# Delta rule: the gate's statistics of three of its four sources made beside the recurrence

## The reference, cut to what matters

```python
def _per_head_stats(x):
    mean = jnp.mean(x, -1, keepdims=True)
    var = jnp.var(x, -1, keepdims=True)
    am = jnp.mean(jnp.abs(x), -1, keepdims=True)
    l2 = jnp.sqrt(jnp.sum(x * x, -1, keepdims=True))
    return jnp.concatenate([mean, var, am, l2], -1)
...
delta_out, _S = _delta_rule_chunkwise(q, k, v_direct, beta)
local_short = _fir_conv(v_direct, fir_short_w)
local_long = _fir_conv(v_direct, fir_long_w)
stats = jnp.concatenate([_per_head_stats(local_short), _per_head_stats(local_long),
                         _per_head_stats(delta_out), _per_head_stats(v_direct)], -1)
gate_in = jnp.concatenate([hs_exp, stats], -1)
h1 = jax.nn.gelu(gate_in @ mlp1_w.T + mlp1_b)
logits = h1 @ mlp2_w.T + mlp2_b
```

## Time and profile before

| | us |
|---|---|
| median of three launches | 3241.55 |
| lowest and highest of them | 3233.91 and 3244.31 |
| the profiled launch | 3234.41 |
| its span, first to last instruction | 3233.1 |
| TensorE busy in it | 2661.0 (82%) |
| VectorE busy in it | 2186.1 (68%) |
| ScalarE busy in it | 1378.1 (43%) |
| GpSimd busy in it | 572.6 (18%) |

### The profile page before, as it was taken

One profiled execution on the slowest core, in us unless ns is written; L12 is line 12 of the kernel. 1 busy time (PEld: TensorE's weight loads), 2 busy tenths in 40 slices (PEclk: granted clock), 3 DMA queues, 4 the chain that ended last, 5 costly groups with the idle time before them and its releaser, 6 DMA issues.

```text
span 3233.1 us, 41018 instructions
## 1 busy us (share of the span) xinstructions
PE 2661.0 (82%) x15734; PEld 1723.3 (53%) x15734; DVE 2186.1 (68%) x4115; ACT 1378.1 (43%) x2436; POOL 572.6 (18%) x482
## 2 busy tenths in 40 slices
PE   5789897886788678989788878869878989778888
PEld 1256674453485323766454448659845455444554
DVE  6987888998999899988699876651174243552331
ACT  5533336563552453333365555441134335334342
POOL 2700001115690054000011108200010100000000
PEclk8999997787887689989788779869989999789899
DMA  3000001110000000000211110007400000000000
GB/s 146 0 1 1 1 1 34 33 37 8 1 1 1 0 1 0 1 33 1 69 34 33 27 59 1 1 1 227 132 1 2 0 2 1 7 1 1 1 2 7
DMA packets 51924, 73.18 MB, mean 23 GB/s; under 512 B 5776, under 2 KB 41360, under 8 KB 51088
## 3 DMA queue, kind: packets, MB, share of 16 engines
q1 hardware_dynamic: 51728, 70.56, 7.2%
HBM read 52.32 MB, written 1.44 MB: 17 GB/s over the span
## 4 chain that ended last, share of the span: by engine, by line
PE 39%; DVE 16%; issue 5%; ACT 3%; POOL 1%; DMA 0%; SPq 0%; DVEq 0%; POOLq 0%; ACTq 0%
PE ps L108 35%; PE ps L111 3%; DVE wide_q L138 3%; DVE conv L135 2%; DVE state L141 2%; DVE inverse L147 1%; DVE qk L129 1%; POOL long L129 1%; DVE stream_a L132 1%; DVE outT L144 1%; DVE stats L153 1%; DVE x L129 1%; DVE turned L129 0%; DMA turned<-conv 0%; ACT L120 0%
## 5 line engine op out<-in xcount | busy, mean ns | idle before, releaser
L108 PEld LDWEIGHTS ps<-held_ffn,hidden 128*128 128x128 f32 x2304 | 298.4, 191 | 160.1 <-issue 108.6
L121 ACT ACTIVATE grown<-ps,bias_grown 128x512 f32<-128x512 f32 x288 | 198.0, 688 | 324.9 <-PE ps L108 318.1
L108 PE MATMUL ps<-held_ffn,hidden 128*128 128x128 f32 x2304 | 306.6, 276 | 22.1 <-DVE hidden L135 22.1
L129 POOL TENSOR_TENSOR qk<-conv,held_const 128x512 f32<-128x512 f32 x64 | 93.0, 1455 | 1030.2 <-DVE conv L135 1030.2
L135 DVE SCALAR_TENSOR_TENSOR conv<-conv_in,held_l1a,conv 128x512 f32<-128x512 f32 x288 | 207.5, 738 | 29.4 <-ACT conv L121 26.0
L129 POOL TENSOR_TENSOR long<-long,product 128x512 f32<-128x512 f32 x136 | 199.3, 1502 | 155.5 <-ACT product L121 154.9
L135 DVE SCALAR_TENSOR_TENSOR hidden<-ps,bias_kept,grown 128x512 f32<-128x512 f32 x288 | 210.7, 745 | 3.3
L132 DVE TENSOR_SCALAR grown<-grown,bias_fallen 128x512 f32<-128x512 f32 x288 | 139.2, 484 | 83.7 <-ACT grown L121 82.8
L138 DVE TENSOR_REDUCE wide_q<-ps 128x4 f32<-128x512 f32 (+1 forms) x128 | 114.4, 954 | 95.6 <-PE ps L108 95.6
L129 POOL TENSOR_TENSOR part<-state,c_rows 128x512 f32<-128x512 f32 x128 | 162.4, 1297 | 85.8 <-issue 48.5
L159 POOL MEMSET wide_q<- 128x1536 f32 x8 | 11.0, 1378 | 925.5 <-ACT rstd L121 925.5
(11 more groups left out here) (440 smaller groups left out, 5820.2 us busy)
## 6 DMA issues: line engine op xcount, KB each, us to landing
ring<-lags SPq DMA_DIRECT2D x64, 512.0 KB, 4.5
turned<-conv SPq DMA_DIRECT2D x256, 64.0 KB, 2.0
held_ffn<-in_ffn SPq DMA_DIRECT2D x1, 4690.0 KB, 18.7
held_l1a<-in_l1a SPq DMA_DIRECT2D x2, 2120.0 KB, 15.7
held_l3f<-in_l3f SPq DMA_DIRECT2D x1, 2824.0 KB, 12.2
held_rows<-in_rows SPq DMA_DIRECT2D x1, 1044.5 KB, 8.0
out<-x SPq DMA_DIRECT2D x4, 256.0 KB, 2.6
held_const<-in_const SPq DMA_DIRECT2D x1, 785.0 KB, 4.9
```

Source lines behind the costliest of these rows:

```text
L108: return self.sent(self.real.matmul(out, lhsT, rhs, **kw), cost, 0.15)
L121: return self.sent(self.real.activation(out, a, func, **kw), cost)
L129: return self.vector(self.real.tensor_tensor(out, a, b, op), columns(out))
```

## The change

The statistics are made source by source, 512 elements for each partition at a time instead of 2048. Those of slots 0, 3 and 1 become programs of their own for VectorE (`early_vector`, a second lane of the planner on that engine) and ScalarE (`early_scalar`, behind the products of the long filter). They wait for `taken_v`, `taken_f` and `long_kept`, and no longer for `out`. Only slot 2 stays behind `out`. For each source there are five large VectorE instructions (two sums, the difference, two more sums) and four small ones, and two squares on ScalarE. All sources share one buffer `off` and one buffer `square`, so a source waits for the one before it. The Gelu's output gets a buffer of its own (`hidden`), and buffers that the recurrence no longer reads are overlaid by the statistics, for which `k`, `kb` and the others change places. TensorE gets one wait more (`var_e`) ahead of turning the statistics.

```diff
+              "mean_e size_e mean_kept_e middled_e sq0_e sq1_e l2_in_e var_e "
...
+        yield from gate.early_scalar(act)
...
-    gate = gate_sources(m, st, x, L, o, Arena(m, mark, a.end - mark), H, D)
+    gate = gate_sources(m, st, x, L, o, Arena(m, mark, a.end - mark), mark, 4 * (SEQS * (PAD + T) + 2 * TOK), H, D)
     st.xs += 1
-    return L.run(PE=tensor, ACT=scalar, ACT_2=products, DVE=vector, POOL=pool)
-
-
-def gate_sources(m, st, x, L, o, a, H, D):
+    return L.run(PE=tensor, ACT=scalar, ACT_2=products, DVE=vector, DVE_2=gate.early_vector, POOL=pool)
+def gate_sources(m, st, x, L, o, a, mark, dead, H, D):
     w = m.w
     s = L.s
     G = NT * H
     S = 4
-    b = a.many(mean=[P, S, G], centred=[P, S, G, D], square=[P, S, G, D], stat=[P, NT, H, S * S],
-               statT=[H * S * S, TOK], logit=[P, G, S], peak=[P, G], total=[P, G], mixed=[P, G, D], sq=[P, G],
-               rms=[P, G], oT=[P, TOK])
-    hidden = b.square[:, :, :, :].rearrange("p s g d -> p s (g d)")
+    FIRST, LAST = (0, 3, 1), 2
+    b = a.many(stat=[P, NT, H, S * S], mean=[P, S, G], off=[P, G, D], square=[P, G, D])
+    assert a.at - mark <= dead
...
+    def stats_of(ve, k, q, n):
+        mean = b.mean[:, k, :]
+        ve.tensor_reduce(mean, src[:, k, :, :], X, ALU.add).then_inc(q.mean)
+        ve.tensor_reduce(stat(2)[:, k, :], src[:, k, :, :], X, ALU.add, apply_absolute_value=True).then_inc(q.size)
+        yield ve.wait_ge(q.mean, 2 * n + 1)
+        ve.tensor_scalar(mean, mean, 1.0 / D, None, ALU.mult).then_inc(q.mean)
+        yield ve.wait_ge(q.size, 2 * n + 1)
+        ve.tensor_scalar(stat(2)[:, k, :], stat(2)[:, k, :], 1.0 / D, None, ALU.mult).then_inc(q.size)
+        yield ve.wait_ge(q.mean, 2 * n + 2)
+        ve.tensor_copy(stat(0)[:, k, :], mean).then_inc(q.mean_kept)
+        ve.tensor_tensor(b.off[:, :, :], src[:, k, :, :], mean.unsqueeze(2).to_broadcast([P, G, D]), ALU.subtract
+                         ).then_inc(q.middled)
+        yield ve.wait_ge(q.sq0, n + 1)
+        ve.tensor_reduce(stat(3)[:, k, :], b.square[:, :, :], X, ALU.add).then_inc(q.l2_in)
+        yield ve.wait_ge(q.sq1, n + 1)
+        ve.tensor_reduce(stat(1)[:, k, :], b.off[:, :, :], X, ALU.add).then_inc(q.var)
+        yield ve.wait_ge(q.var, 2 * n + 1)
+        ve.tensor_scalar(stat(1)[:, k, :], stat(1)[:, k, :], 1.0 / D, None, ALU.mult).then_inc(q.var)
+    def squares_of(act, k, q, n):
+        act.activation(b.square[:, :, :], src[:, k, :, :], ACT.Square).then_inc(q.sq0)
+        yield act.wait_ge(q.middled, n + 1)
+        act.activation(b.off[:, :, :], b.off[:, :, :], ACT.Square).then_inc(q.sq1)
+    def early_vector(ve):
+        yield ve.wait_ge(s.taken_v, 1)
+        yield ve.wait_ge(s.taken_f, 1)
+        yield ve.wait_ge(s.long_kept, 1)
+        for n, k in enumerate(FIRST):
+            if n:
+                yield ve.wait_ge(s.var_e, 2 * n)
+            yield from stats_of(ve, k, early, n)
+    def early_scalar(act):
+        yield act.wait_ge(s.taken_v, 1)
+        yield act.wait_ge(s.taken_f, 1)
+        yield act.wait_ge(s.long_kept, 1)
+        for n, k in enumerate(FIRST):
+            if n:
+                yield act.wait_ge(s.l2_in_e, n)
+            yield from squares_of(act, k, early, n)
     def vector(ve):
         yield ve.wait_ge(m.load["rows"], 16)
         yield ve.wait_ge(s.out, 1)
-        yield ve.wait_ge(s.taken_f, 1)
-        yield ve.wait_ge(s.long_kept, 1)
-        mean = b.mean[:, :, :].rearrange("p s g -> p (s g)")
-        ve.tensor_reduce(mean, groups_, X, ALU.add).then_inc(s.mean)
-        ve.tensor_reduce(stat(2), src, X, ALU.add, apply_absolute_value=True).then_inc(s.size)
-        yield ve.wait_ge(s.mean, 1)
-        ve.tensor_scalar(b.mean[:, :, :], b.mean[:, :, :], 1.0 / D, None, ALU.mult).then_inc(s.mean)
-        yield ve.wait_ge(s.size, 1)
-        ve.tensor_scalar(stat(2), stat(2), 1.0 / D, None, ALU.mult).then_inc(s.size)
-        yield ve.wait_ge(s.mean, 2)
-        ve.tensor_copy(stat(0), b.mean[:, :, :]).then_inc(s.mean_kept)
-        ve.tensor_tensor(all_(b.centred[:, :, :, :]), groups_,
-                         mean.unsqueeze(2).to_broadcast([P, S * G, D]), ALU.subtract).then_inc(s.middled)
-        yield ve.wait_ge(s.sq0, 1)
-        ve.tensor_reduce(stat(3), b.square[:, :, :, :], X, ALU.add).then_inc(s.l2_in)
-        yield ve.wait_ge(s.sq1, 1)
-        ve.tensor_reduce(stat(1), b.centred[:, :, :, :], X, ALU.add).then_inc(s.var)
-        yield ve.wait_ge(s.var, 1)
-        ve.tensor_scalar(stat(1), stat(1), 1.0 / D, None, ALU.mult).then_inc(s.var)
+        yield ve.wait_ge(s.var_e, 2 * len(FIRST))
+        yield from stats_of(ve, LAST, late, 0)
...
-        act.activation(b.square[:, :, :, :], src, ACT.Square).then_inc(s.sq0)
-        yield act.wait_ge(s.middled, 1)
-        act.activation(b.centred[:, :, :, :], b.centred[:, :, :, :], ACT.Square).then_inc(s.sq1)
+        yield act.wait_ge(s.l2_in_e, len(FIRST))
+        yield from squares_of(act, LAST, late, 0)
...
+        yield pe.wait_ge(s.var_e, 2 * len(FIRST))
...
-        m.weave.add({name: chain(layers[st.name], name) for name in ("PE", "ACT", "ACT_2", "DVE", "POOL", "SP")},
+        m.weave.add({name: chain(layers[st.name], name) for name in ("PE", "ACT", "ACT_2", "DVE", "DVE_2", "POOL", "SP")},
```

14 lines of the change are left out of this document (9 added, 5 removed).

## The result

| | before | after |
|---|---|---|
| median | 3239.14 us (3233.91 to 3245.40, 6 runs) | 3260.78 us (3258.80 to 3265.17, 6 runs) |
| profiled launch | 3234.41 us, span 3233.1 | 3260.48 us, span 3258.9 |

The ratio of after to before is 1.0070, 95% interval 1.0057 to 1.0083: the change makes the kernel about 22 us slower. The forecast was 3267 us, within 3243 to 3291. The two profiled launches lie 26.1 us apart, where the sum of the forecast had 29.

What follows compares the result with a forecast made beforehand. TensorE bounds recurrence and gate; turning stream A's statistics decides when the block ends. The stretch to it becomes 41.6 + 16.2 = 57.8 us in each pair, +29 us in all: 3234.4 + 29 + 4 = 3267 us, range 3243 to 3291.

Steps and rivals of the forecast that it cites:

- The bound passes from TensorE to VectorE: Recurrence: 38.1 us of VectorE work plus 4 us idle make 42.1 us, 4.8 us of VectorE work a step.
- the changes between 32 and 128 partitions: Recurrence: VectorE alternating between `adj` and statistics costs 2 us for each pair, bounds 0 and 4.
- From the last step to the turning: Behind stream A's last `adj`: TensorE's row of both streams, 16.2 us, is what turning stream A's statistics waits for.
- The rival on the clock: Recurrence: TensorE's clock falls to 1.2 GHz, eight steps take 46.4 us, +45 us in all, 3279 us; chance 0.19.
- this part gets 5 us shorter in the second pair: Last step to turning, second pair: 20.8 us before, 5 us shorter now, against a recurrence 20 us longer.
- TensorE near half busy: Expected sign in the recurrence: TensorE near half busy, at a clock of 1.00, or 0.50 if the first rival holds.
- The gate unchanged: Gate's two layers, from the turn to stream B's logits: 35 to 36 us as before.
- the gate at 2.4 GHz: Gate: unbroken TensorE work ahead raises the clock and it stays, -33 us against +29, 3230 us; chance 0.09.
- a gate under 30 us: Sign of being wrong: the gate itself gets shorter than 30 us, which would be the clock.
- The levels of the second pair: New interleaving beside GpSimd's long filter: taken as 0, bounds -7.5 and +7.5 us; a difference here signals being wrong.
- the forecast's +4 for the median: Whole kernel: 4 us added to the profiled-launch sum of 3263.4 us to forecast the median, 3267 us.
- The edits at no cost: ScalarE's twelve squares hide in recurrence idle time; dropped table loads, the `var_e` wait and buffer places change nothing.

Runs made afterwards that it cites:

- e6: Changed kernel in its exact instruction order, early VectorE and ScalarE statistics work on 2 of 32 channels; 3236.02 us, ratio 0.9991 to the kernel before.
- e3: Changed kernel with one source (long filter, slot 1) made early instead of three, the other three behind the recurrence; 3273.80 us, ratio 1.0115 to the kernel before.
- e5: Changed kernel with three more unread VectorE sums for each early source, 18 more in each pair; 3278.09 us, ratio 1.0129 to the kernel before.
- e11: Changed kernel with variance as mean square minus squared mean, three large VectorE instructions a source instead of five; 3259.22 us, ratio 1.0078 to the kernel before.
- e1: Kernel before with each of a stream's five large VectorE instructions cut in four at its place, nothing moved; 3242.06 us, ratio 1.0017.
- e2: Kernel before with only the delta rule's buffers kbn, kb, k, qn and kn at the change's places; 3238.23 us, ratio 1.0005.
- e8: Kernel before with variance as mean square minus squared mean, three large VectorE instructions a stream instead of five; 3230.48 us, ratio 0.9977.
- e9: Kernel before with two unread matmuls more in each pair, put into TensorE's holes ahead of the gate; 3236.38 us, ratio 1.0000.
- e10: Kernel before with e8's variance plus e9's two unread matmuls in each pair; 3226.37 us, ratio 0.9973.

## Why the prediction was right

**The bound passes from TensorE to VectorE: right.** The recurrence took 40.6 and 43.5 us against 42.1. VectorE's busy time is 35.31 and 35.52 us, where the sum had 38.1. Its idle time is 5.3 and 8.0, where the sum had 4 with 7.0 as the upper bound, so in the second pair that bound was passed. The two errors cancel in part. The first has a size: 24 small instructions took about 0.08 us instead of 0.13, 1.2 us in all (the 0.13 came from rows of four times as many elements, 128x64 instead of 128x16). Of the 2 us for the changes between 32 and 128 partitions little is left: 15.0 + 30 x 0.60 + 24 x 0.08 are 34.9 of the 35.3 us. And e6 has all these changes in a recurrence of 26.3 and 29.9 us, no longer than before, though VectorE had room there to hide them. The runs with little, usual and more work are the direct proof of the step: in the first pair the recurrence grows by what VectorE is given.

The Trainium skill, "Perfetto Trace Analysis", section "Optimizing Scalar/DVE Operations", says that breaking up instructions may let work be completed sooner if VectorE is not saturated but causes bubbles on other engines. Both conditions seemed to be there: VectorE at 83%, and TensorE waiting for it behind the recurrence. The trace of after shows what the sentence leaves open: the pieces went to a stretch whose own idle time on VectorE was 5.3 and 7.0 us, and 21 us don't go into that.

**From the last step to the turning: right in kind, too small in size.** TensorE is what the turning waits for, as forecast. The term was 16.2 us for TensorE's row; from the row's start it measured 17.3 in the first pair (1025.84 to 1043.18) and 19.0 in the second. The mis-sized part is the 32 small matmuls of both streams: 2 x 3.7 = 7.4 us were taken from a row at full clock, and they took 10.71 and 11.11 us, the first 3.5 and 3.1 of them at full clock and the rest at half. The rival on the clock reckoned that at half clock they "slow down by a fifth"; from start to start they take 0.21 us instead of 0.11, nearly twice as long, so at half clock throughout they would take about 13.7 us (estimate, 64 x 0.213). For the input's matmuls of both streams the sum had 8.8 us, and they took 4.40 + 2.74 = 7.1 in the first pair. In the second pair it is 5.47 + 3.01 = 8.5. The prediction also says that this part gets 5 us shorter in the second pair, from 20.8. It counted the recurrence before at its work and its idle time, 22.0 us; to stream B's last `adj` it took 30.6 us and the part behind it 12.2. So that part got 6.4 us longer, and the recurrence 12.9 and not 20 longer; the sum of the two doesn't depend on where the line is drawn.

**The clock in the recurrence: the rival came in part.** It forecast 0.50 throughout. The clock was 0.76 in the first pair and 0.63 in the second, where TensorE was busy 39.48 of 43.6 us. The stretch of the second pair is 62.2 us instead of 57.8, 1.4 of it in the recurrence and the rest in the row behind. Adding work cost only 6.5 us for 9.8 there, with the clock going from 0.63 up to 0.71. So the two engines share the bound in that pair, and how much belongs to which can't be read off a single trace. "TensorE near half busy" was wrong in both pairs (34.77 of 40.60 us, 39.48 of 43.60): at the lower clock the same matmuls fill most of the longer step.

**The gate unchanged: wrong, by 15.4 us.** The step that failed is to take the gate at 35 to 36 us as before, for the reason that "the clock stays at 0.50 through 34.70 us of almost unbroken work". That row shows that unbroken work in the gate doesn't raise the clock. It doesn't show what happens if the clock is already up when the gate begins, and that is now the case: it comes up in the row ahead of the gate and is kept for some of it. The rival "the gate at 2.4 GHz" had the right mechanism and place, and gave it 33 us where it was worth 15.4, since the clock doesn't stay. The prediction named a gate under 30 us as a sign of being wrong, and it came in both pairs; so did in part another, a difference in the second pair's levels. The runs behind it say how uncertain the gain is: with after's TensorE order and no hole in the row ahead, the gate is 28.6 and 27.5 in after, 27.5 and 28.7 with more work, 33.5 and 27.5 with little, 33.3 and 33.2 with the other variance; with the hole of 10.87 us it is 36.3.

**The levels of the second pair: the bound was needed.** They were taken at 0 with 7.5 as bound, and cost 5.6 us. GpSimd in order of time, beside them (columns as in the earlier trace rows):

```profile
1991.07 1.27 POOL L129 TENSOR_TENSOR long<-long,product 128x512 f32<-128x512 f32 x1 [7.27 <-ACT product L121]
...
2014.87 1.27 POOL L129 TENSOR_TENSOR long<-long,product 128x512 f32<-128x512 f32 x1 [2.98 <-ACT product L121]
...
2038.71 1.27 POOL L129 TENSOR_TENSOR long<-long,product 128x512 f32<-128x512 f32 x1 [3.02 <-ACT product L121]
```

The stall of 7.56 us is still there with 7.27, and two of 3 us are new; before, none behind the large one was over 1 us. GpSimd's idle time in the filter goes from 14.0 to 19.6 us, as much as the levels. It repeats: the levels of the second pair took 172.7 to 173.2 us in the five kernels with after's order there (after, e3, e5, e6, e11), and 167.1 to 167.6 in the six with the old one (before, e1, e2, e8, e9, e10).

**The sum.** Forecast +29, measured +26 between the profiled launches: +33.3 in the stretch (29.1 forecast), -15.4 in the gate (0), +5.6 in the levels (0), +2.6 elsewhere. The number was near because errors of both signs met, and that part of it is luck: without the gate's gain the same sum would have come out at about +41, against the +29 forecast. The direction rests on the term that was right in kind, work put on an engine without room for it. The medians differ by less than the profiled launches, 21.6 us, since the forecast's +4 for the median was the case before (3239.14 against 3234.41) and not after (3260.78 against 3260.48).

**The edits at no cost: right.** The new places in memory cost nothing that can be measured (e2, ratio 1.0005). The squares on ScalarE stayed under cover: it is busy 8.29 of 40.60 us.

## What to carry to other kernels

- Work moved beside a loop is hidden only as far as the engine it goes to is idle inside that loop. Here that was 5 to 7 us of idle time for 21 us of work, though the engine that bounded the loop was another one.
- If a wait is on an engine, look first for work that needn't be done: leaving two of five large instructions out of the statistics made the kernel 0.23% faster, and moving three quarters of them made it 0.70% slower.
- A stretch on TensorE at half clock has two prices. When the work ahead of it changes, cost it at both, and don't count a gain in a recurrence as kept until the stretch behind it has been measured too.

## What the runs showed of the hardware

- In a row of TensorE work without a gap the clock went both ways: from 1.00 to 0.50 in the small matmuls of `adj,mixT`, and back to 1.00 in the input's matmuls behind them. From there it was kept into the gate, which before had run at 0.50 nearly from its start: 5.43 us for the first fifteen instructions at 1.00, where they had taken 10.43 at 0.50. How long it stays differs between kernels whose TensorE order is the same (gate of 28.6 or 33.3 us in the first pair).
- Passes of `adj,mixT`, 32 columns each, start 0.11 us apart at full clock (32 take 3.65 us) and 0.21 apart at half: even such short matmuls take nearly twice as long. In after, 64 of them took 10.71 and 11.11 us, since about half of them still ran at full clock.
- Small VectorE instructions (128 x 16, float32) start 0.08 us apart when they follow each other, and large ones of 128 x 512 start 0.60 apart though each lasts 0.68.
